# Four of eight first-norm tiles turned by a transposing DMA instead of by TensorE, with the norm weight applied on Pool

## The reference, cut to what matters

```python
# attention over stored patterns; x: [8192, 2048], 16 heads of 128
y      = layernorm(x)
normed = rms(y, norm_query_w)                 # the "first norms" of this change
q      = (normed @ W_in.T).reshape(.., 16, 128) @ W_q.T
k, v   = stored_patterns @ W_k.T, stored_patterns @ W_v.T   # per head: 1024 x 128
p      = softmax(sigmoid(beta) * q @ k.T)
x      = x + rms(p @ v, norm_retrieved_w) + y
# feed-forward, int8 weights with a scale for each column
z      = layernorm(x)
x      = x + ((silu(z @ w_gate * s_gate) * (z @ w_up * s_up)) @ w_down) * s_down
```

## Time and profile before

| | |
|---|---|
| median of 3 runs | 1626.28 us |
| profiled execution's own time | 1625.37 us |
| its span on the slowest core, first to last instruction | 1623.7 us |
| spans of the 8 cores | 1619.0 to 1623.7 us |
| granted TensorE clock | 0.998 to 0.999 on all cores |
| PE busy | 1583.5 us, 98% of the span |
| DVE, ACT, POOL busy | 321.1, 304.3, 203.9 us (20%, 19%, 13%) |
| L892 (gate, up), L1032 (down) on PE | 880.4 and 440.0 us |
| L351 transposes on PE | 256 of them, 20.3 us |

### The profile page before, as it was taken

The page is one execution under the profiler, slowest core; times in us unless marked ns, Lnnn a source line. Parts: engine busy times, 40 slices in busy tenths (PEclk is TensorE's granted clock), DMA queues, the critical chain, the costliest instruction groups (busy, mean ns, idle before and its releaser), DMA issues.

```text
span 1623.7 us, 20461 instructions; the slowest of 8 cores (1619.0 to 1623.7 us)
## 1 busy us (share of the span) xinstructions
PE 1583.5 (98%) x8232; PEld 763.4 (47%) x8395; DVE 321.1 (20%) x610; ACT 304.3 (19%) x388; POOL 203.9 (13%) x424
## 2 busy tenths in 40 slices
PE   4999999999999999999999999999999999999998
PEld 3555556444444444444444444444444444444443
DVE  4355465382110000000000000000000200201102
ACT  5677657221110000000000000000000100100200
POOL 4232243111110000000000000000010000000000
PEclk9999999999999999999999999999999999999999
DMA  8974665465442222222222222221252522523411
GB/s 179 175 144 93 143 170 157 157 232 198 145 151 78 78 78 78 78 78 78 78 78 78 78 78 75 70 73 70 90 181 78 182 78 78 177 72 99 159 52 53
DMA packets 52083, 181.44 MB, mean 112 GB/s; under 512 B 5904, under 2 KB 6416, under 8 KB 48656
## 3 DMA queue, kind: packets, MB, share of 16 engines
q0 software_dynamic: 38592, 135.94, 28.3%
q1 hardware_dynamic: 8640, 35.72, 6.1%
q10 hardware_dynamic: 4752, 8.40, 1.9%
HBM read 126.17 MB, written 16.78 MB: 88 GB/s over the span
## 4 chain that ended last, share of the span: by engine, by line
PE 96%; DMA 2%; issue 1%; DVE 0%; POOL 0%; ACT 0%; SPq 0%; DVEq 0%; POOLq 0%; ACTq 0%
PE PS L892 54%; PE PS L1032 27%; PE PS L549 6%; PE PS L630 3%; PE PS L586 3%; DMA arena<-winT 1%; DMA arena<-x 1%; PE PS L351 1%; PE PS L518 0%; PE PS L511 0%; POOL arena L342 0%; PE PS L570 0%; POOL arena L94 0%; ACT arena L592 0%; DVE arena L366 0%
## 5 line engine op out<-in xcount | busy, mean ns | idle before, releaser
L892 PE MATMUL PS<-arena 128*128 128x512 bf16 x4013 | 880.4, 379 | 4.4
L892 PEld LDWEIGHTS PS<-arena 128*128 128x128 bf16 x4096 | 400.4, 98 | 481.6
L1032 PE MATMUL PS<-arena 128*128 128x512 bf16 x2007 | 440.0, 379 | 2.2
L1032 PEld LDWEIGHTS PS<-arena 128*128 128x128 bf16 x2048 | 200.4, 98 | 241.6
L912 DVE SCALAR_TENSOR_TENSOR arena<-PS,cols_s,arena 128x1024 bf16<-128x1024 f32 (+1 forms) x78 | 85.1, 1092 | 741.8 <-PE PS L892 730.1
L909 ACT ACTIVATE arena<-PS,cols_s 128x1024 bf16<-128x1024 f32 (+1 forms) x78 | 75.0, 961 | 784.4 <-PE PS L892 764.8
L94 POOL DMA_DIRECT2D arena<-wg x78 | 41.4, 531 | 793.1 <-PE PS L892 723.5
L592 ACT ACTIVATE arena<-PS 128x1024 bf16<-128x1024 f32 x128 | 128.0, 1022 | 48.2 <-PE PS L586 47.9
L549 PE MATMUL PS<-arena 128*128 128x512 bf16 x490 | 117.4, 380 | 2.5 <-DMA arena<-winT 2.0
L1018 DVE TENSOR_TENSOR arena<-PS,arena 128x512 f32<-128x512 f32 (+1 forms) x33 | 22.3, 674 | 392.3 <-PE PS L1032 392.3
L1009 ACT ACTIVATE arena<-arena,c_s 128x512 f32<-128x512 f32 x32 | 25.5, 811 | 322.9 <-DVE arena L1021 308.0
(11 more groups left out here) (89 smaller groups left out, 386.8 us busy)
## 6 DMA issues: line engine op xcount, KB each, us to landing
arena<-wg POOLq DMA_DIRECT2D x78, 512.0 KB, 3.5
arena<-wu POOLq DMA_DIRECT2D x78, 512.0 KB, 4.3
arena<-wd POOLq DMA_DIRECT2D x64, 512.0 KB, 3.6
arena<-x SPq DMA_DIRECT2D x16, 1024.0 KB, 7.4
arena<-winT POOLq DMA_DIRECT2D x31, 512.0 KB, 7.1
x1sp<-arena SPq DMA_DIRECT2D x8, 1024.0 KB, 4.7
arena<-x1sp ACTq DMA_DIRECT2D x32, 256.0 KB, 6.1
out<-arena SPq DMA_DIRECT2D x31, 256.0 KB, 5.1
```

The source lines that it names most:

```text
L892: f = lambda En, n=n, hf=hf, hc=hc, b0=b0, w=w: En.matmul(bank(b0 + n), w[:, hc * 128:(hc + 1) * 128], x1T[hf][:, hc, :], start=(hc == 0), ...
L1032: return lambda En: En.matmul(bank(j), fuse[:, ic, j * 128:(j + 1) * 128], wdb[(q * 16 + g) % 8][:, c * 512:(c + 1) * 512], start=(ic == 0 ...
```

## The change

The four later tiles are no longer turned by PE. After `ln_apply`, SP issues one transposing DMA for the whole tile, from `ns[j % 2]` straight to its place in `nqT[1]`, at (b+2, 0) in the emitted order. At (b+2, 3) Pool multiplies the turned tile in place by the norm weight, broadcast over the 128 columns of each block, as one instruction of 128x2048. `ns` is free when the DMA has landed; the projection waits for Pool's multiplication. The DMAs of all four tiles come from SP's queue, with two semaphores in turn. The first four tiles are made as before.

```diff
+    def turned(self, lane, dst, src, *toks):
+        lane.wait(*toks)
+        self.n += 16
+        lane.ops.append(lambda En, d=dst, s=src, h=self.sem: En.dma_start_transpose(out=d, in_=s).then_inc(h, 16))
         return (self.sem, self.n)
...
+        s_xt = [Slot(sem("dxt%d" % i)) for i in range(2)]
...
+            def nqT_tile(j):
+                dst = nqT[1][:, :, (j % 4) * 128:(j % 4 + 1) * 128]
+                t = s_xt[j % 2].turned(sp, dst, ns[j % 2], t_nqs[j])
+                nsfree[j % 2] = t
+
+            def nqT_weighted(j):
+                dst = nqT[1][:, :, (j % 4) * 128:(j % 4 + 1) * 128]
+                t = nsfree[j % 2]
+                t = pool.tick(lambda En: En.tensor_tensor(dst, dst, nqw.unsqueeze(2).to_broadcast([128, EC, 128]), ALU.mult),
+                              t, t_cols)
+                t_nqT[1][0].append(t)
+                t_nqT[1][8].append(t)
...
                     at(b + 2, 0, lambda j=j: apply(j))
-                    at(b + 2, 2, lambda j=j: nqT_part(j, 0, 8, 6))
-                    at(b + 3, 2, lambda j=j: nqT_part(j, 8, 8, 6))
+                    at(b + 2, 0, lambda j=j: nqT_tile(j))
+                    at(b + 2, 3, lambda j=j: nqT_weighted(j))
```

More of the change, by code:

```diff
@@ L94, in dma @@
         lane.ops.append(lambda En, d=dst, s=src, h=self.sem: En.dma_start(out=d, in_=s).then_inc(h, 16))
+        return (self.sem, self.n)
+    def turned(self, lane, dst, src, *toks):
+        lane.wait(*toks)
+        self.n += 16
+        lane.ops.append(lambda En, d=dst, s=src, h=self.sem: En.dma_start_transpose(out=d, in_=s).then_inc(h, 16))
         return (self.sem, self.n)
@@ L1068, in _build_nc @@
         outs_fast = layer(False)
-        slots_all = [s_cols, s_sc, s_mats, s_wr, s_sd] + s_x + s_w + s_pat + s_spill + s_wd + s_xg + s_xr + s_out
+        slots_all = [s_cols, s_sc, s_mats, s_wr, s_sd] + s_x + s_w + s_pat + s_spill + s_wd + s_xg + s_xt + s_xr + s_out
         ends = [(e.sem, e.n) for e in (pe, act, dve, pool, sp) if e.n] + [(e.sem, e.n) for e in slots_all]
```

## The result

The change makes the kernel slower. Its median is 1644.89 us over 7 runs, against 1626.28 us before. The ratio is 1.0087, with a 95% interval of 1.0066 to 1.0108: about 14 us more (0.0087 x 1626). I had forecast 1624.4 us in a range of 1622.5 to 1639.

What follows compares the result with a forecast made beforehand. PE, busy for 98% of the span, was taken to bound the kernel. Removed transposes gain 1.9 us and the new waits cost 0, so the median of 1626.3 becomes 1624.4 us, in a range of 1622.5 to 1639.

Steps and rivals of the forecast that it cites:

- 3.5 plus half of 3.1, 5.0 us: Transposing DMA on SP: 3.5 us lower bound from plain DMAs, plus half of one winT load's 3.1 us, 5.0 us.
- the slack of 2.3: Tile 7 before slot 15's projection: 11.45 us available, 9.1 needed for DMA and multiplication, 2.3 us spare.
- Who is queued behind the new waits: Work behind the new waits on Pool, SP and ACT claimed hidden: cost 0, up to 1 us if a cover fails.
- on DVE nothing waits any more: DVE, in the cost of the new waits: claimed no waiting there, as part of a cost of 0.
- the threshold: ACT's squares need ns 17 us or more after the DMA's issue; only a longer DMA would hold the exponentials.
- Pool's two-input operation doesn't slow it: DVE beside Pool's multiplication: claimed no slowdown, since L642 takes 424 to 426 ns with or without L711 on Pool.
- Rival A: DMA passes 4 KB pieces one after another, 25.8 us; PE stalls 18.5 us in slot 15; 1643 us, chance 0.26.
- D: Rival: DMA broken into 262,144 single 2-byte elements a tile, 255 us each; near 2560 us, chance 0.03.
- The slots without transposes: Slots 4 to 14 on PE, once transposes are gone: all forecast 8.2 to 8.35 us long.
- my term: PE's gain from removed transposes in eight slots, after a returning bank wait: 0.24 us a slot, 1.9 us in all.
- 4.1 forecast: Pool's added 128x2048 multiplication per tile: 4.1 us, between bounds of 2.05 and 5.4.
- The deadline of tile 7: Only tile 7 has one: PE's first projection reading it, at 160.56 us, 11.45 us after Pool's ln_apply ends.

Runs made afterwards that it cites:

- e5: Kernel before, with transposing DMAs added into unused space during the gate matmuls: full tile alone 4.4 us, beside two casting loads 11.1 us.
- e12: Kernel before, with gate-phase transposing DMAs each beside one thing: 4.2 us alone, 6.1 beside a plain load, 7.4 beside winT, 11.6 beside two casting loads.
- e11: Changed kernel with Pool's multiplication directly behind the DMA's issue, holding Pool's loads, and tile 7 turned by PE: 1625.19 us, ratio 1.0000.
- e4: Kernel before, PE's transposes kept, with the norm weight of tiles 4 to 6 moved to Pool: 1626.16 us, ratio 1.0001.
- e1: Changed kernel with Pool's multiplications of tiles 4 to 6 moved behind the next tile's root, two slots later: 1641.13 us, ratio 1.0096.
- e13: e11 without the transposing DMAs in the second layer copy, behind a branch never taken: 1625.51 us, ratio 0.9992.
- e8: Changed kernel with the early squares' own scratch, multiplications of tiles 4 to 6 two slots later, and tile 7 turned by PE: 1642.25 us, ratio 1.0094.
- e9: Changed kernel with Pool's multiplication directly behind the DMA's issue, so Pool's loads wait with it: 1633.13 us, ratio 1.0049.

## Why the prediction was wrong

**What failed: the DMA's length, "3.5 plus half of 3.1, 5.0 us".** The 3.5 was good (4.4 alone). The sharing was not. I charged half of one load's engine time as if both streams only took turns. Measured: 7.4 us beside one load of winT, 11.6 beside two loads, 9.2 to 17.4 on the slowest core of the kernel after. The term was mis-sized by a factor of two for tile 7 (4.2 us, which alone used up the slack of 2.3) and of three for the others, where I had named only one load and there were two and more. I also had the load's own slowdown at nothing: winT takes up to 13.4 us. The Trainium skill, "Advanced Engine Details and Errata", section X-Bar Transpose (TRN2), says that a transposing DMA runs as fast as an ordinary one; e5 has 4.4 us for the DMA alone against 2.9 for a plain copy of the same bytes, half as long again, and in e12's mixes it is 7.4 and 11.6. The Trainium skill's figure of 1309 ns for a block by DMA, in "VectorE: DVE Perf Modes", section The three transpose paths, does not multiply here: one block takes 2.2 us to landing, sixteen take 4.4.

**What failed: "Who is queued behind the new waits", costed at 0.** I listed the loads behind Pool's wait, and not the next tile's root, which stands behind it as well, nor x on SP, which waits for one of these loads and so ran into the next DMA, nor what waits for the root: DVE's shift, and behind this in DVE's order the cast that frees PE's bank. At 5 us that would have held; at 17 it costs 3.3 us. I wrote that on DVE nothing waits any more: it waits 7.66 us there. For ACT I had the threshold right (a DMA of about 17 us holds the exponentials) and then left it, because I gave only tile 7 a deadline. Tile 6 has one as well: slot 12.

**"Pool's two-input operation doesn't slow it"** is wrong for one kind: DVE's 128x2 L278, 0.16 us otherwise, took 3.58 us exactly beside Pool's L394 (145.06, above). My rows had tested other forms on both sides. The Trainium skill, "SBUF — State Buffer", section SBUF: two separate sides, describes the port pair that the two engines share as an exclusive lock for the whole instruction; this row agrees, while L663, 0.42 us beside L394 at 117.64, kept its time. It did not end a wait of PE here, since PE waited for ACT.

**Rival A** forecast 1643 us, near the 1644.89. Its mechanism is refuted: the pieces do not pass one at a time (e5), and slot 15 is one of three places, with 2.5 us where A had 18.5. That its number is right is chance. D is refuted too: 2080 packets a tile, not 262,144.

**What held.** The slots without transposes: 8.2 us. The gain was a little larger than my term, 0.33 us a slot (2.0 us for six groups in e11) where I took 0.24; for eight it would be 2.6 and not 1.9. Pool's multiplication: 3.61 us against 4.1 forecast, and hidden when its inputs are there (e4). The deadline of tile 7 and who would wait for it.

**What I had not seen at all:** the lower clock behind waits of about 3 us, 3.3 us of the 12.9; and the tail, 2.0 us. For the slowest core the account is then: slots 4 to 15 110.56 - 100.57 = 10.0, tail 1340 - 1338 = 2, in all 12.0 of 1636.0 - 1623.7 = 12.3 us.

**Open.** Why the mix in the attention goes as far as 31 us, when the worst that I made by itself was 11.7, was not isolated. Three or more loads at once, and x or wr among them, are a difference that the traces show, but cores 4 and 5 of e1 had the same loads at the same distances, with 9.5 and 24.8 us. What the other cores move in that time was not looked at. A kernel with the squares' own scratch and Pool holding its loads was not run.

## What to carry to other kernels

A transposing DMA is priced by what else moves in its time, not by its bytes: put it where no casting load runs, or keep the turning on an engine that has room. When an engine gets a new wait of uncertain length, write down everything behind it in its own order for the worst length, then who waits for each of these, down to the bound engine. And look at the end of the program too: e11 and e13 differ only in code that never runs, and by 1.7 us there.

## What the runs showed of the hardware

- With nothing beside it, a 128x2048 bf16 tile is turned from SBUF to SBUF in 4.2 to 4.4 us, in 256-byte packets, 2080 of them; a 128x128 block in 2.2.
- Transposing DMAs and casting loads slow each other: 4.4 to 11.6 us, and the loads from 3.5 and 4.2 to 9.9 and 10.9. A plain load beside it costs it less (6.1) and is itself 4.2.
- In the attention the same DMA beside the same loads took 9.5 us on one core and 24.8 on another (e1, cores 4 and 5).
- The issue of a transposing DMA holds SP: 1.32 to 12.98 us in the kernel after, 16.20 in e8 (core 7).
- After idle times of PE of 3.29, 2.52 and, in e9, 5.70 us, the clock fell to the 1.2 GHz level for some microseconds (0.50 in e9 from 163.54 to 167.20); after 2.93 us (slot 12) the next window shows 1.00 still.
- Two programs that differ by three transposing DMAs in code that never runs (e11, e13) differ by 1.7 us between the last matmul and the end, with 3 instruction fetches there against 1 or 2.
